# Splitting the attention probabilities in one operation per engine instead of two halves

## The chip, the core and the metric

The kernel runs on one core of one Trainium2 chip. The metric is device time in microseconds (us) of one execution, the median of several runs. Engines are called by the profile's names: PE (TensorE, matrix products), PEld (its weight loads), DVE (VectorE), ACT (ScalarE), POOL (GpSimd), SP (SyncE, here the queue that issues the DMAs).

## The reference, cut to what matters

64 graphs of 128 nodes with 512 features pass through two masked attentions with 8 heads (first nodes to edges, then edges to nodes, with the incidence matrix transposed and as it is), layer norms, a feed-forward network of width 2048 and a last layer norm:

```python
def _attn(q, k, v, mask):
    scores = jnp.einsum('bhid,bhjd->bhij', qh, kh) * SCALE
    scores = jnp.where(mask[:, None] > 0, scores, -jnp.inf)
    w = jax.nn.softmax(scores, axis=-1)
    out = jnp.einsum('bhij,bhjd->bhid', w, vh)
...
edge_features = _attn(eq, nk, nv, n2e_mask)
edge_features = _ln(edge_features + pe, norm1_g, norm1_b)
...
node_updates = _attn(nq, ek, ev, incidence_matrix)
node_features = _ln(pe + node_updates, norm2_g, norm2_b)
h = jax.nn.gelu(_lin(node_features, ffn_w1, ffn_b1), approximate=False)
out = _ln(node_features + _lin(h, ffn_w2, ffn_b2), norm3_g, norm3_b)
```

All of it is in float32. The kernel reaches the accuracy by splitting operands into a high and a low part and summing three (or five) products of the parts.

## The kernel before

The 64 graphs are worked on in 16 groups of 4. Each attention pass goes over the 16 groups, and each group takes 4 steps (`u` = 0 to 3): a step is one pair of heads for the 4 graphs, so a pass has 64 steps and the two passes 128, numbered n. The probabilities of a step are a 128x1024 tile: 8 blocks (4 graphs, 2 heads) of 128x128. Of the 16 groups of a pass the first two and the last two are written out, and the 12 between them run as 6 iterations of a loop of two groups, which is 8 steps (`over_groups`, L109). The feed-forward pass follows the two attention passes.

Every engine has its own program, and semaphores tie them. Nothing orders the work but these programs, each in the order in which it is written.

- PE in a step: keys, queries (24 products), the weighing of the values with the probabilities of two steps earlier (`weigh`, L861), transposes of the finished group (`turn`, L843), values (12 products, L877), and the scores of the step (L928), which need the split queries `q_lo`. One `weigh` of each group also waits for the low part of the values, which POOL makes.
- DVE in a step: the mask and the maximum of the 8 score blocks of the step before (`mask_and_maximum`, L766), the rest of a value (L742), once per group the centring of the norm (L684), the low part of the probabilities (`probabilities_low`, L775), the low parts of keys and queries (L747, L750, L755), and the sum of the weighed values with the tokens (`add_weighed`, L690 to L712).
- ACT in a step: 8 exponentials with the row sums (L526), the high part of the probabilities (`probabilities_high`, L533), high parts of keys and queries (L513 to L520), of the next group's source (L549), the copies of turned blocks (L483), the high part of a value (L509).
- POOL in a step: the middle and low part of a value (`value_low`: L627, L629), low parts of the source (L642), the bias of the tokens (`add_bias`, L647). Each of these reads SBUF.
- SP: `turn_probabilities` (L378 to L386) waits until the earlier step's probabilities are weighed, then until both halves of `p_hi` are there, and issues its transposing DMA; then the same for `p_lo`.

The split of the probabilities: `probs` (float32) is copied to `p_hi` (float16) by ACT, and DVE computes `p_lo = probs - p_hi`. Both are done in two halves of 128x512, and DVE may start its first half when ACT has made its first half:

```python
act.wait_ge(exped, UNIT * n + 4 * h + 4)
nc.scalar.copy(p_hi[:, 4 * h:4 * h + 4, :], probs[:, 4 * h:4 * h + 4, :]).then_inc(p_hi_ready, 1)
...
dve.wait_ge(p_hi_ready, 2 * n + h + 1)
nc.vector.tensor_tensor(p_lo[:, 4 * h:4 * h + 4, :], probs[:, 4 * h:4 * h + 4, :], p_hi[:, 4 * h:4 * h + 4, :],
                        ALU.subtract).then_inc(p_lo_ready, 1)
```

The first half's copy waits for the first 4 exponentials, the second's for all 8. In the loop over steps both halves come after all 8 exponentials; only after the last step of the second pass (`ends`) ACT runs 4 exponentials, a half, 4 exponentials, a half. `weights_high` of the feed-forward weights (`high`, L219) and their low parts (`low`, L226) are a copy and a subtraction of 128x1024 each.

Of the kernel before, what the change touches and what calls it, by code (L numbers as in the profile page):

```python
# [46 lines left out]
ALU = mybir.AluOpType  # L47
# [26 lines left out]
UNIT = GB * 2  # L74
# [5 lines left out]
def wait(engine, semaphore, value):  # L80

    if isinstance(value, int) and value <= 0:
        return
    engine.wait_ge(semaphore, value)
# [144 lines left out]
def attention_passes(nc, ctx, m, block, passes, feed_forward, nodes_features, residual, identity_in):  # L229
# [147 lines left out]
    def turn_probabilities(sp, n):  # L377

        wait(sp, weighed, n)
        sp.sem_inc(sp_steps, 1)  # L380
        sp.wait_ge(p_hi_ready, 2 * n + 2)
        sp.sem_inc(sp_steps, 1)
        sp.dma_start_transpose(pt_hi[:], p_hi[:].rearrange("p j i -> p (j i)")).then_inc(hi_turned, 16)
        sp.wait_ge(p_lo_ready, 2 * n + 2)
        sp.sem_inc(sp_steps, 1)
        sp.dma_start_transpose(pt_lo[:], p_lo[:].rearrange("p j i -> p (j i)")).then_inc(lo_turned, 16)  # L386

# [100 lines left out]
    def _(act):  # L488
# [37 lines left out]
                nc.scalar.activation(probs[:, j, :], probs[:, j, :], ACT.Exp, bias=minus_max[:, j:j + 1], scale=-1.0,  # L526
                                     accum_out=row_sum[:, side, j:j + 1]).then_inc(exped, 1)

        def probabilities_high(n, h):
            if h == 0:  # L530
                wait(act, hi_turned, 16 * n)
            act.wait_ge(exped, UNIT * n + 4 * h + 4)
            nc.scalar.copy(p_hi[:, 4 * h:4 * h + 4, :], probs[:, 4 * h:4 * h + 4, :]).then_inc(p_hi_ready, 1)  # L533

        def split_queries(g):

# [18 lines left out]
        def body(g, parity, before, own, after):  # L555
            if ends(g):
                n = C * g - 1
                for h in range(2):
                    exponentials(n, 1, h)
                    probabilities_high(n, h)  # L560
                feed_forward.high(act, 2)
                feed_forward.high(act, 3)
                return
            for u in range(C):
                n = C * g + u - 1
                first = starts(g) and u == 0
                if u == 2 and own != after:

                    act.wait_ge(projected, value_place(g, 3) + 1)
                    if after == 1:  # L570
                        weights_high(1, "v")
                    else:
                        feed_forward.high(act, 0)
                        feed_forward.high(act, 1)
                if u == 0 and starts(g):
                    value_high(0, 0, 0)
                    value_high(0, 0, 1)
                if not first:
                    exponentials(n, (u - 1) % 2, 0)
                    exponentials(n, (u - 1) % 2, 1)  # L580
                    probabilities_high(n, 0)
                    probabilities_high(n, 1)
                key_high(g, own, u)
                query_high(g, own, u)
                if u < 2:
                    split_source(g, parity, range(2 * u, 2 * u + 2))
                if u == 0 and not below(g, 2):
                    copy_turned(act, g - 2, own, 3)
                if u == 2 and not starts(g):
                    copy_turned(act, g - 1, before, 0)  # L590
                    copy_turned(act, g - 1, before, 1)
                if u == 3:
                    if own == 1 and after == 1:
                        split_queries(g + 1)
                    if not starts(g):
                        copy_turned(act, g - 1, before, 2)
                    if at(g, last_group - 1):
                        copy_turned(act, g - 1, before, 3)
                if u < 2:
                    value_high(g, parity, u + 2)  # L600
                elif not at(g, last_group - 1):
                    value_high(g + 1, 1 - parity, u - 2)
            if own != after and after == 1:

                weights_high(1, "k")
                weights_high(1, "q")
                split_queries(g + 1)
# [107 lines left out]
    def _(dve):  # L715
# [42 lines left out]
        def mask_and_maximum(n, first):  # L758
            if first is not None:
                dve.wait_ge(mask_ready, first + 1)  # L760
            wait(dve, p_lo_ready, 2 * n)
            for h in range(2):
                gate(dve, scored, 2 * n + h + 1, dve_scratch[:, h:h + 1])
                for j in range(4):
# [3 lines left out]
                        in1=mask[:, 2 * h + j // 2, :], scale=-SCALE, scalar=LARGEST, op0=ALU.add, op1=ALU.min,  # L768
                        accum_out=minus_max[:, 4 * h + j:4 * h + j + 1]).then_inc(masked, 1)

        def probabilities_low(n, h):
            if h == 0:
                wait(dve, lo_turned, 16 * n)
            dve.wait_ge(p_hi_ready, 2 * n + h + 1)
            nc.vector.tensor_tensor(p_lo[:, 4 * h:4 * h + 4, :], probs[:, 4 * h:4 * h + 4, :], p_hi[:, 4 * h:4 * h + 4, :],  # L775
                                    ALU.subtract).then_inc(p_lo_ready, 1)

        def first_queries():

# [5 lines left out]
        def body(g, parity, before, own, after):  # L785
            if ends(g):
                n = C * g - 1
                mask_and_maximum(n, None)
                for h in range(2):
                    probabilities_low(n, h)  # L790
                feed_forward.low(dve, 2)
                feed_forward.low(dve, 3)
                return
            for u in range(C):
# [18 lines left out]
                if u == 2 and not starts(g):  # L813
                    centre(dve, g - 1, 1 - parity)
                if not first:
                    probabilities_low(n, 0)
                    probabilities_low(n, 1)
                key_low(g, own, u)
                query_low(g, own, u)
                if u == 2 and own != after:  # L820
# [607 lines left out]
```

## Time and profile before

| | us |
|---|---|
| median of 3 runs | 2949.8 (2947.25 to 2950.87) |
| the profiled execution | 2950.69 |
| its span (first to last instruction) | 2948.9 |
| around the span | 1.8 |
| attention passes, from the trace's start | 0 to about 1525 |

The granted TensorE clock was 0.994 of full speed over the span. Busy times are in the first part of the profile's page; the wait views say which engine stood idle before an instruction, and what ended it; the timeline view lists instructions with start and length, equal neighbours merged (`x2`), and in brackets the idle time just before them.

### The profile page before, as it was taken

The numbers are of one execution on the slowest core, as the hardware profiler recorded it, in microseconds if no ns is written. First come the engines' busy times: TensorE is split into PE (matmuls) and PEld (weight loads), VectorE is DVE, ScalarE is ACT, GpSimd is POOL, SyncE is SP. The second block draws the span as 40 slices with busy tenths as digits, with TensorE's granted clock in tenths as the row PEclk, the third lists the DMA queues.
The fourth block names the chain that finished last, engine by engine and source line by source line (L and its number), as shares of the span: only waits on it lengthen the run. The fifth ranks groups of instructions, "written<-read, shape, count | busy, mean of one in ns | idle before, by whom it ended". The sixth has DMA issues, their size and how long they took to land.

```text
span 2948.9 us, 54948 instructions
## 1 busy us (share of the span) xinstructions
PE 2864.6 (97%) x17920; PEld 2393.6 (81%) x17920; DVE 1761.7 (60%) x5972; ACT 1551.1 (53%) x4138; POOL 1118.1 (38%) x1115
## 2 busy tenths in 40 slices
PE   9999999999899999999979999999999999999997
PEld 7888877888788888888868888888888888888886
DVE  7888888888888888888873333322333332233333
ACT  6777777777787787787864222222222222222221
POOL 3443534344355645546522322333312333321233
PEclk9999999999999999999999999999999999999998
DMA  7554444444566766756664101011101011110101
GB/s 198 125 115 120 118 111 118 114 125 109 149 151 157 180 162 157 175 147 168 162 170 134 57 29 53 33 57 57 57 30 55 33 52 57 57 57 28 58 14 57
DMA packets 487992, 295.43 MB, mean 100 GB/s; under 512 B 278912, under 2 KB 410112, under 8 KB 487808
## 3 DMA queue, kind: packets, MB, share of 16 engines
q1 hardware_dynamic: 487808, 293.49, 37.5%
q14 instruction: 131, 1.07, 0.1%
q8 instruction: 53, 0.87, 0.1%
HBM read 159.21 MB, written 67.11 MB: 77 GB/s over the span
## 4 chain that ended last, share of the span: by engine, by line
PE 80%; DVE 8%; issue 5%; ACT 4%; POOL 1%; DMA 0%; DVEq 0%; SPq 0%; ACTq 0%; POOLq 0%
PE proj L1326 23%; PE proj L877 23%; PE score L1340 12%; PE proj L1340 12%; PE score L928 4%; PE att_out L861 4%; ACT att_probs L526 2%; DVE normed L703 2%; PE att_turn L843 2%; ACT turned L483 1%; DVE att_p_lo L775 1%; DVE att_q_lo L755 1%; DVE att_stats L708 1%; DVE att_k_lo L750 1%; ACT att_p_hi L533 0%
## 5 line engine op out<-in xcount | busy, mean ns | idle before, releaser
L1259 DVE TENSOR_TENSOR hidden_lo<-hidden,hidden_hi 128x512 fp32r<-128x512 f32 x256 | 188.2, 735 | 935.0 <-ACT hidden_hi L1111 935.0
L1118 ACT ACTIVATE hidden<-proj,ffn_bias 128x512 f32<-128x512 f32 x256 | 176.8, 691 | 996.3 <-PE proj L1326 996.3
L526 ACT ACTIVATE att_probs<-att_probs,att_minus_max 128x128 f32<-128x128 f32 x1024 | 397.7, 391 | 169.8 <-DVE att_minus_max L766 169.8
L775 DVE TENSOR_TENSOR att_p_lo<-att_probs,att_p_hi 128x512 f16<-128x512 f32 x256 | 232.5, 947 | 150.1 <-ACT att_p_hi L533 150.1
L101 POOL TENSOR_TENSOR pool_scratch<-pool_scratch 128x1 f32<-128x1 f32 x144 | 38.1, 264 | 698.5 <-DVE ffn_moments L1199 396.4
L1178 POOL TENSOR_TENSOR source_lo<-source_raw,source_hi 128x512 fp32r<-128x512 f32 x60 | 79.3, 1322 | 449.6 <-ACT source_hi L1129 449.6
L766 DVE CUSTOM_DVE_ANT_0 att_probs<-score,att_mask 128x128 f32<-128x128 f32 x1024 | 226.7, 287 | 18.8 <-PE score L928 9.7
L877 PE MATMUL proj<-weight_v_hi,source_hi 128*128 128x512 f32 x512 | 216.1, 422 | 9.9 <-DVE weight_v_lo L724 7.2
L483 ACT ACTIVATE turned<-att_turn,att_shift,att_gain 128x128 f32<-128x128 f32 x512 | 193.0, 458 | 59.2 <-PE att_turn L843 59.2
L642 POOL TENSOR_TENSOR source_lo<-source_raw,source_hi 128x512 fp32r<-128x512 f32 x128 | 163.0, 1296 | 126.7 <-ACT source_hi L549 126.7
L877 PE MATMUL proj<-source_hi,weight_k_hi 128*128 128x512 f32 x512 | 201.0, 393 | 2.3 <-DVE weight_k_lo L724 2.3
L877 PE MATMUL proj<-weight_v_hi,source_lo 128*128 128x512 f32 x512 | 202.4, 395 | 0.0
L877 PE MATMUL proj<-weight_v_lo,source_hi 128*128 128x512 f32 x512 | 201.2, 393 | 0.0
L877 PE MATMUL proj<-source_lo,weight_k_hi 128*128 128x512 f32 x512 | 200.7, 392 | 0.0
L877 PE MATMUL proj<-source_hi,weight_k_lo 128*128 128x512 f32 x512 | 199.3, 389 | 0.0
L1326 PE MATMUL proj<-source_hi,w_lo 128*128 128x512 f32 x512 | 199.2, 389 | 0.0
L1326 PE MATMUL proj<-source_hi,w_hi 128*128 128x512 f32 x512 | 199.2, 389 | 0.0
L1326 PE MATMUL proj<-source_lo,w_hi 128*128 128x512 f32 x512 | 199.2, 389 | 0.0
L526 ACT ACTIVATION_READ_ACCUMULATOR att_probs<-att_probs,att_minus_max 128x1 f32 x1024 | 193.0, 188 | 0.0
L861 PEld LDWEIGHTS att_out<-att_v,att_pt_hi 128*128 128x128 f16 x3072 | 149.2, 98 | 44.5 <-issue 44.5
L647 POOL TENSOR_TENSOR att_tokens<-att_tokens,bias_row 128x512 f32<-128x512 f32 x128 | 181.4, 1417 | 1.0 <-DMA att_tokens<-in_x 1.0
L861 PE MATMUL att_out<-att_v,att_pt_hi 128*128 128x64 bf16 x3072 | 163.9, 193 | 9.1 <-POOL att_v L629 9.1
(149 smaller groups left out, 8358.9 us busy)
## 6 DMA issues: line engine op xcount, KB each, us to landing
att_tokens<-in_x SPq DMA_DIRECT2D x128, 256.0 KB, 3.0
edges_t<-turned SPq DMA_DIRECT2D x64, 256.0 KB, 2.5
source_raw<-edges_t SPq DMA_DIRECT2D x16, 1024.0 KB, 6.1
att_query_raw<-in_x_t SPq DMA_DIRECT2D x16, 1024.0 KB, 6.8
nodes_t<-turned SPq DMA_DIRECT2D x64, 256.0 KB, 2.8
source_raw<-nodes_t SPq DMA_DIRECT2D x16, 1024.0 KB, 6.1
normed<-nodes SPq DMA_DIRECT2D x16, 1024.0 KB, 5.6
ffn_weight_raw<-in_x SPq DMA_DIRECT2D x16, 1024.0 KB, 8.1
```

Source lines behind the costliest of these rows:

```text
L483: last = nc.scalar.activation(turned[:, b % 2, c, :], turn_bank[:, c * P:(c + 1) * P], ACT.Identity, bias=shift_column[own][:, c:c + 1], s ...
L526: nc.scalar.activation(probs[:, j, :], probs[:, j, :], ACT.Exp, bias=minus_max[:, j:j + 1], scale=-1.0, accum_out=row_sum[:, side, j:j + 1 ...
L642: nc.gpsimd.tensor_tensor(source_lo[1 - parity][:, c, :], source_raw[:, c, :], source_hi[1 - parity][:, c, :].bitcast(F32), ALU.subtract). ...
L647: nc.gpsimd.tensor_tensor(pair(tokens, u), pair(tokens, u), bias_v[:, u * P:(u + 1) * P].rearrange("p (o d) -> p o d", o=1).to_broadcast([ ...
L766: nc.vector.tensor_tensor_reduce(out=probs[:, 4 * h + j, :], in0=score_bank[h][:, j * P:(j + 1) * P], in1=mask[:, 2 * h + j // 2, :], scal ...
L775: nc.vector.tensor_tensor(p_lo[:, 4 * h:4 * h + 4, :], probs[:, 4 * h:4 * h + 4, :], p_hi[:, 4 * h:4 * h + 4, :], ALU.subtract).then_inc(p ...
L861: last = nc.tensor.matmul(out, p, value, start=(i == 0), stop=(i == len(products) - 1))
L877: last = nc.tensor.matmul(bank[:], stationary, moving, start=(c == 0 and i == 0), stop=(c == C - 1 and i == 2))
L1118: nc.scalar.activation(hidden[:, c % 2, :], up_bank[c % 2][:], ACT.Gelu, bias=bias_1[:, c:c + 1]).then_inc(activated, 1)
L1259: nc.vector.tensor_tensor(hidden_lo[:, c % 2, :], hidden[:, c % 2, :], hidden_hi[:, c % 2, :].bitcast(F32), ALU.subtract).then_inc(hidden_ ...
L1326: last = nc.tensor.matmul(up_bank[c % 2][:], w, s, start=(i == 0), stop=(i == len(products) - 1))
L1340: last = nc.tensor.matmul(down_bank[b][:], h, w, start=(c == 0 and i == 0), stop=(c == FC - 1 and i == 2))
```

## The change

The copy to `p_hi` becomes one 128x1024 operation on ACT, and the subtraction one 128x1024 operation on DVE. Each semaphore counts one per step instead of two, and all waits on them are renumbered. The copy waits for all 8 exponentials; the subtraction waits for the whole copy. In `ends` all 8 exponentials now come ahead of the copy.

```diff
-        sp.wait_ge(p_hi_ready, 2 * n + 2)
+        sp.wait_ge(p_hi_ready, n + 1)
...
-        sp.wait_ge(p_lo_ready, 2 * n + 2)
+        sp.wait_ge(p_lo_ready, n + 1)
...
-        def probabilities_high(n, h):
-            if h == 0:
-                wait(act, hi_turned, 16 * n)
-            act.wait_ge(exped, UNIT * n + 4 * h + 4)
-            nc.scalar.copy(p_hi[:, 4 * h:4 * h + 4, :], probs[:, 4 * h:4 * h + 4, :]).then_inc(p_hi_ready, 1)
+        def probabilities_high(n):
+
+            wait(act, hi_turned, 16 * n)
+            act.wait_ge(exped, UNIT * n + UNIT)
+            nc.scalar.copy(p_hi[:], probs[:]).then_inc(p_hi_ready, 1)
...
                 for h in range(2):
                     exponentials(n, 1, h)
-                    probabilities_high(n, h)
+                probabilities_high(n)
...
-                    probabilities_high(n, 0)
-                    probabilities_high(n, 1)
+                    probabilities_high(n)
...
-            wait(dve, p_lo_ready, 2 * n)
+            wait(dve, p_lo_ready, n)
...
-        def probabilities_low(n, h):
-            if h == 0:
-                wait(dve, lo_turned, 16 * n)
-            dve.wait_ge(p_hi_ready, 2 * n + h + 1)
-            nc.vector.tensor_tensor(p_lo[:, 4 * h:4 * h + 4, :], probs[:, 4 * h:4 * h + 4, :], p_hi[:, 4 * h:4 * h + 4, :],
-                                    ALU.subtract).then_inc(p_lo_ready, 1)
+        def probabilities_low(n):
+
+            wait(dve, lo_turned, 16 * n)
+            dve.wait_ge(p_hi_ready, n + 1)
+            nc.vector.tensor_tensor(p_lo[:], probs[:], p_hi[:], ALU.subtract).then_inc(p_lo_ready, 1)
...
-                for h in range(2):
-                    probabilities_low(n, h)
+                probabilities_low(n)
...
-                    probabilities_low(n, 0)
-                    probabilities_low(n, 1)
+                    probabilities_low(n)
```

## Rows read from the trace of the kernel before

**Rows 1.** The page's first part: busy us (share of the span) xinstructions.

```profile
PE 2864.6 (97%) x17920; PEld 2393.6 (81%) x17920; DVE 1761.7 (60%) x5972; ACT 1551.1 (53%) x4138; POOL 1118.1 (38%) x1115
```

**Rows 2.** Waits of DVE, 40 to 590 us: us in total, times, longest us.

```profile
DVE att_p_lo L775 <- ACT att_p_hi L533: 53.6, 35, 1.8
DVE att_dve_scratch L92 <- issue: 15.1, 5, 3.1
```

**Rows 3.** Waits of PE, 40 to 590 us.

```profile
PE score L928 <- DVE att_q_lo L755: 11.3, 5, 2.4
PE att_out L861 <- POOL att_v L629: 3.7, 4, 0.9
```

**Rows 4.** Waits of PE, 960 to 1400 us.

```profile
PE att_out L861 <- POOL att_v L629: 4.6, 5, 0.9
...
PE score L928 <- DVE att_q_lo L755: 3.0, 5, 0.7
```

**Rows 5.** Groups by line and form, 100 to 1620 us: xcount | busy us, mean ns.

```profile
L533 ACT CAST att_p_hi<-att_probs 128x512 f16<-128x512 f32 x242 | 136.6, 612 | 0.1
...
L219 ACT CAST w_hi<-ffn_weight_raw 128x1024 fp32r<-128x1024 f32 x10 | 10.5, 1047 | 1.6 <-DMA ffn_weight_raw<-in_w 1.6
...
L226 DVE TENSOR_TENSOR weight_k_lo<-ffn_weight_raw,weight_k_hi 128x1024 fp32r<-128x1024 f32 x2 | 2.5, 1225 | 1.0 <-ACT weight_k_hi L219 0.9
```

**Rows 6.** Timeline of ACT, a step of the loop and the last step: start us, us.

```profile
212.30 0.19 ACT L526 ACTIVATION_READ_ACCUMULATOR att_probs<-att_probs,att_minus_max 128x1 f32 x1
212.39 1.13 ACT L533 CAST att_p_hi<-att_probs 128x512 f16<-128x512 f32 x2
...
1522.68 0.19 ACT L526 ACTIVATION_READ_ACCUMULATOR att_probs<-att_probs,att_minus_max 128x1 f32 x1
1522.90 0.62 ACT L533 CAST att_p_hi<-att_probs 128x512 f16<-128x512 f32 x1
```

**Rows 7.** Timeline of DVE and POOL, first pass, steps 16 to 19 and 23.

```profile
213.10 1.46 DVE L775 TENSOR_TENSOR att_p_lo<-att_probs,att_p_hi 128x512 f16<-128x512 f32 x2 [1.76 <-ACT att_p_hi L533]
...
218.61 1.29 POOL L647 TENSOR_TENSOR att_tokens<-att_tokens,bias_row 128x512 f32<-128x512 f32 x1
...
225.13 1.45 POOL L647 TENSOR_TENSOR att_tokens<-att_tokens,bias_row 128x512 f32<-128x512 f32 x1
...
225.37 2.36 DVE L775 TENSOR_TENSOR att_p_lo<-att_probs,att_p_hi 128x512 f16<-128x512 f32 x2
...
236.68 2.55 DVE L775 TENSOR_TENSOR att_p_lo<-att_probs,att_p_hi 128x512 f16<-128x512 f32 x2 [1.76 <-ACT att_p_hi L533]
...
236.95 1.73 POOL L647 TENSOR_TENSOR att_tokens<-att_tokens,bias_row 128x512 f32<-128x512 f32 x1
...
248.18 1.93 DVE L775 TENSOR_TENSOR att_p_lo<-att_probs,att_p_hi 128x512 f16<-128x512 f32 x2 [1.29 <-ACT att_p_hi L533]
...
297.36 2.27 DVE L775 TENSOR_TENSOR att_p_lo<-att_probs,att_p_hi 128x512 f16<-128x512 f32 x2 [0.75 <-ACT att_p_hi L533]
...
297.51 1.57 POOL L629 TENSOR_TENSOR att_v<-att_v_rest,att_v 128x512 bf16<-128x512 f32 x1
```

**Rows 8.** Timeline of DVE, second pass, steps 86 to 88.

```profile
1039.19 0.29 DVE L766 CUSTOM_DVE_ANT_0 att_probs<-score,att_mask 128x128 f32<-128x128 f32 x1 [0.20 <-issue]
...
1043.33 1.30 DVE L775 TENSOR_TENSOR att_p_lo<-att_probs,att_p_hi 128x512 f16<-128x512 f32 x2 [1.75 <-ACT att_p_hi L533]
...
1057.24 2.17 DVE L775 TENSOR_TENSOR att_p_lo<-att_probs,att_p_hi 128x512 f16<-128x512 f32 x2 [1.47 <-ACT att_p_hi L533]
...
1068.36 1.46 DVE L775 TENSOR_TENSOR att_p_lo<-att_probs,att_p_hi 128x512 f16<-128x512 f32 x2 [1.76 <-ACT att_p_hi L533]
```

**Rows 9.** Timeline of DVE and PE between the passes, and SP after the last step.

```profile
748.75 2.49 DVE L724 TENSOR_TENSOR weight_v_lo<-att_weight_v_raw,weight_v_hi 128x512 fp32r<-128x512 f32 x4
...
749.54 0.47 PE L877 MATMUL proj<-weight_v_hi,source_hi 128*128 128x512 f32 x1 [2.77 <-issue]
...
1529.50 1.35 SPq L213 DMA_DIRECT2D ffn_weight_raw<-in_w  x2
```

## The prediction

> **What bounds the kernel now.** I read the shares first, then the waits of DVE and PE in stretches of the attention passes, then single steps in the timeline. PE is busy for 97% of the span [rows 1], so PE looks like the only bound. The waits say otherwise for the first pass. From 40 to 590 us DVE waits for nothing but ACT's copy `p_hi` (35 times, 53.6 us) and a pause at each turn of the loop, 5 times up to 3.1 us [rows 2]; no row says that it waits for PE. ACT's exponentials in turn start on DVE's maxima. So here DVE and ACT run a ring of their own: maxima, exponentials, `p_hi`, `p_lo`, `k_lo`, `q_lo`, `add_weighed`, the next maxima. PE follows it: once in each turn of the loop it waits for `q_lo` (5 times, 11.3 us) and once more for POOL's `att_v`, which starts from DVE's `v_rest` (4 times, up to 0.9 us) [rows 3]. What the ring loses in 8 steps, PE loses at its next such wait. In the second pass the same two waits come 5 times each, but shorter (3.0 and 4.6 us) [rows 4], and DVE does wait for scores: at 1039.19 for 0.20 us [rows 8] (the row says issue, but this is the first use of a score bank). There only what is lost after the last such wait counts.
>
> **What the change removes, adds and moves.** Per step it takes away one ACT and one DVE instruction and the overlap between the engines.
>
> ACT. The pair of copies takes 1.13 us [rows 6], one 128x1024 copy to a 4-byte type 1.05 [rows 5]; I take that for the float16 copy, since the 128x512 copy costs 0.61 [rows 5] and two of them overlap by 0.09. Saved: 0.08. But the copy now waits for the last exponential, whose row sum is read out at the end. Without that wait the first copy starts 0.09 after the start of the readout (212.30, 212.39); where the wait was there already, after the last step, 0.22 (1522.68, 1522.90) [rows 6]. Added: 0.13. So `p_hi` is whole 0.05 later than before. Behind it on ACT stand `k_hi`, `q_hi`, the source's high part and the copies of turned blocks, 0.05 later each; SP's first transposition already waited for both halves and is 0.05 later too. No row has PE waiting for a transposition [rows 3, 4], so that costs nothing.
>
> DVE. Two undisturbed halves take 1.30 us (1043.33) [rows 8], one 128x1024 subtraction 1.225 [rows 5]: 0.07 saved. But `p_lo` starts later: before, the copy's start + 0.61 + 0.10 = 0.71 (212.39 to 213.10) [rows 5 to 7]; now 0.13 + 1.05 + 0.10 = 1.28 after it, so 0.57 later. With nothing in the way it ends at 0.57 + 1.22 = 1.79 after the old start, against 1.30: 0.49 late. Behind it on DVE stand `k_lo`, `q_lo`, `add_weighed` and the next maxima, and PE's scores wait for `q_lo`.
>
> POOL changes this from step to step. At 225.37 DVE was late for other reasons; POOL's addition (225.13 to 226.58) kept the pair until 227.73 [rows 7], 1.15 after POOL's end. One operation then ends 1.15 - 0.07 = 1.08 after POOL's end. In the loop of the first pass the 8 steps are:
> - Steps 16 and 20 (213.10): the pair took 1.46, slowed by a POOL operation that is over by the new start. New end 1.79: +0.33 each.
> - Steps 17 and 21 (225.37): `p_hi` is long there. -0.07 each.
> - Steps 18 and 22 (236.68): POOL's addition starts 0.27 after the old start and fell between the halves; the pair took 2.55. It now starts before `p_lo` asks, runs its undelayed 1.29 (218.61) to 1.56, and `p_lo` ends at 2.64: +0.09 each.
> - Step 19 (248.18): POOL is still at work when `p_lo` asks. -0.07.
> - Step 23, at the loop's turn (297.36): POOL's subtraction starts 0.15 after the old start. It took 1.57, about 0.4 of it behind the first half, so 1.17 undelayed: 0.15 + 1.17 + 1.08 = 2.40 against 2.27 [rows 7], +0.13; the same step of other rounds starts at a slightly other place and comes out near 0. I take +0.06.
>
> Together 0.66 - 0.14 + 0.18 - 0.07 + 0.06 = 0.69 us in 8 steps. The ring has no wait on PE, so it adds up: five rounds of 8 (steps 8 to 47) 3.45, the steps 1 to 7 by the same rules 0.5, and step 48, whose delay PE meets at `att_v`, 0.33: **4.3 us**.
>
> Rows show POOL's addition stretched from 1.29 to 1.73 behind a half, and DVE's second half stopped behind that addition [rows 7]. By the Trainium skill ("SBUF — State Buffer", Who interferes with whom) the two engines share a port pair that one instruction keeps to its end, which speaks against longer operations: a POOL operation that comes second waits up to 1.22 us instead of 0.6. The trace agrees; by it the sum stays as it is, since in the steps above POOL comes first.
>
> Between the passes PE waits 2.77 us for `weight_v_lo`, whose first quarter DVE ends 0.1 earlier [rows 9]. DVE's steps 49 to 61 gather about 1.1, nearly all of it in steps 56 and 60, where no POOL operation is in the way (+0.49 each); one wait for a score of 0.2 on the way swallows its part: **+0.9**.
>
> Second pass, five rounds. Since the last wait for a score, DVE gathers +0.33 and +0.09 less 0.07 in steps 83 to 85, of which the 0.20 of that wait [rows 8] swallows all but 0.15; step 86 (1043.33) has no POOL in it, +0.49; step 87 (1057.24) about 0; step 88 (1068.36) +0.33, met at `att_v`. 0.97 a round, **4.8 us**.
>
> Last steps: three late `p_lo` of 0.49 with waits between them leave about 0.7; the last step's exponentials, no longer split by a copy, give back 0.3; SP's loads of feed-forward weights at 1529.50 [rows 9] follow: **+0.4**. The feed-forward pass has none of these operations.
>
> Sum: 4.3 + 0.9 + 4.8 + 0.4 = 10.4 us on the profiled 2950.69 (span 2948.9 and 1.8 around it), 2961.1; the median is 0.9 lower, so **2960 us**.
>
> Bounds: if the readout wait costs nothing, open steps lose 0.20 (0.36 without POOL), and the same sum gives about 6.4 us, 2956. If it costs 0.05 more, and the step at the turn loses 0.13 in every round, about 13, 2963. The pause at the turn of the loop, up to 3.1 us [rows 2], is a stop after a branch, and DVE's loop body gets shorter; I allow 0.2 us a turn either way, 2 us over ten turns.
>
> **Rivals.**
> *The slack takes it (no change).* If the ring is pulled back to PE in every group, only the ten waits for `q_lo` [rows 3, 4] count, at about 0.33 each: 3 us, 2953. For it: PE's 97%. Against it: no wait for a score in 550 us of the first pass [rows 2].
> *POOL loses its place (faster).* If POOL's operations at steps 18, 22 and 23 came after `p_lo` asks (later than 0.57 after the old start), the whole operation would run undisturbed and end at 1.79 instead of 2.55 and 2.27: -0.76 twice and -0.48, so a round is 0.69 - 0.18 - 0.06 - 2.0 = -1.55, the first pass about -9; with +2.5 in the second pass (step 87 likewise) and 1.3 at the hand-offs, -5 to -6: 2944. Against it: POOL starts at 0.27 and 0.15 [rows 7], and follows DVE's `v_rest`, not `p_hi`.
> *Instructions saved, nothing lost.* 128 x 0.15 us saved would be up to 19 us; it needs `p_lo` to start where it did, which the new wait forbids. I give it almost nothing.
>
> **How the numbers follow.** A difference under 0.2% (5.9 us) can't be told from no change. Forecast 0.70, the slack 0.19, POOL 0.08, others 0.03. The forecast's own range is 2954 to 2965 with the pause's 2 us; down to 2952 takes in the slack's 2953. Faster by over 0.2% is half of POOL's case and the last rival: 0.06. Within: the slack, the rest of POOL's case and the forecast's low end: 0.25. Slower: 0.69.
>
> **What would show it.** `p_lo` waiting for `p_hi` about 0.57 us longer each time it waits, at 1.22 us or behind POOL; `p_hi` 0.22 after the last readout's start, at 1.05; PE's waits for `q_lo` and `att_v` together about 4 us longer in the first pass and 5 in the second, 0.33 of it at each `att_v`. Wrong if the waits for `q_lo` stay as they are, if POOL's addition comes after `p_lo` at step 18, or if the pause at the loop's turn moves by more than 0.3.

## The result, and the profile after

The changed kernel takes **2958.5 us** in the median of 8 runs (2957.22 to 2961.45), the kernel before 2950.55 in 8 runs beside it (2947.25 to 2952.66): a ratio of **1.003 [1.002, 1.004]**, 8 us slower. The profiled execution took 2957.61 us with a span of 2955.6, so its span is 6.7 us longer than before. The lines that follow are from the profile of the changed kernel; each group of before to which they answer is named.

The page's first part [rows 1]:

```profile
PE 2868.5 (97%) x17920; PEld 2396.0 (81%) x17920; DVE 1720.0 (58%) x5844; ACT 1550.1 (52%) x4010; POOL 1106.7 (37%) x1115
```

DVE is busy for 41.7 us less and ACT for 1.0 us less, with 128 instructions fewer on each, and the kernel is slower. Most of DVE's 41.7 us is not saved work. The merged subtraction is 0.07 us shorter than two undisturbed halves (1.23 against 1.30 [rows 8]), which makes 9 us in 128 steps. The rest is time in which a half waited behind POOL and counted as busy; now DVE is idle instead, as the idle time before the subtraction shows (140.1 us before, 195.8 after).

Groups by line and form, 100 to 1620 us (xcount | busy us, mean ns | idle before) [rows 5]; the first line is of the kernel before:

```profile
L775 DVE TENSOR_TENSOR att_p_lo<-att_probs,att_p_hi 128x512 f16<-128x512 f32 x242 | 218.7, 942 | 140.1 <-ACT att_p_hi L533 140.1
...
L774 DVE TENSOR_TENSOR att_p_lo<-att_probs,att_p_hi 128x1024 f16<-128x1024 f32 x121 | 178.8, 1478 | 195.8 <-ACT att_p_hi L533 195.8
...
L533 ACT CAST att_p_hi<-att_probs 128x1024 f16<-128x1024 f32 x121 | 126.6, 1046 | 10.8 <-ACT att_probs L526 0.4
```

Timeline of ACT in step 16, the last readout and the copy (start us, us) [rows 6]:

```profile
212.99 0.19 ACT L526 ACTIVATION_READ_ACCUMULATOR att_probs<-att_probs,att_minus_max 128x1 f32 x1
213.26 1.05 ACT L533 CAST att_p_hi<-att_probs 128x1024 f16<-128x1024 f32 x1
```

The copy takes the 1.05 us that was forecast. It starts 0.27 after the start of the last readout, where the first half started 0.09 after a readout: a copy that waits for the last row sum starts 0.18 us later.

Timeline of DVE and POOL in steps 16 to 19 [rows 7]; the bracket is the idle time before:

```profile
214.41 1.23 DVE L774 TENSOR_TENSOR att_p_lo<-att_probs,att_p_hi 128x1024 f16<-128x1024 f32 x1 [2.38 <-ACT att_p_hi L533]
...
226.44 2.29 DVE L774 TENSOR_TENSOR att_p_lo<-att_probs,att_p_hi 128x1024 f16<-128x1024 f32 x1
...
238.31 2.02 DVE L774 TENSOR_TENSOR att_p_lo<-att_probs,att_p_hi 128x1024 f16<-128x1024 f32 x1 [2.38 <-ACT att_p_hi L533]
...
237.96 1.28 POOL L646 TENSOR_TENSOR att_tokens<-att_tokens,bias_row 128x512 f32<-128x512 f32 x1
...
249.90 1.23 DVE L774 TENSOR_TENSOR att_p_lo<-att_probs,att_p_hi 128x1024 f16<-128x1024 f32 x1 [1.92 <-ACT att_p_hi L533]
```

In steps 16 and 18 DVE waits 0.62 us longer for `p_hi` (2.38 against 1.76). At step 18 POOL's addition still comes first, and `p_lo` ends 1.09 us after it (239.24 to 240.33). All four steps go as forecast, to 0.05 us.

Waits of DVE, 40 to 590 us (us in total, times, longest) [rows 2], all that the view lists:

```profile
DVE att_p_lo L774 <- ACT att_p_hi L533: 80.0, 36, 2.4
DVE att_dve_scratch L92 <- issue: 14.4, 5, 3.1
```

Waits of PE, 40 to 590 us [rows 3]:

```profile
PE score L924 <- DVE att_q_lo L754: 9.1, 5, 2.1
PE att_out L857 <- POOL att_v L628: 7.0, 9, 1.3
```

Waits of PE, 960 to 1400 us [rows 4]:

```profile
PE att_out L857 <- POOL att_v L628: 7.4, 9, 1.3
...
PE score L924 <- DVE att_q_lo L754: 3.2, 5, 1.4
```

PE's waits for `q_lo` did not grow (9.1 us against 11.3, and 3.2 against 3.0); those for `att_v` did, and come 9 times instead of 4 and 5. Between the passes [rows 9], DVE and PE:

```profile
751.27 1.28 DVE L723 TENSOR_TENSOR weight_v_lo<-att_weight_v_raw,weight_v_hi 128x512 fp32r<-128x512 f32 x2
...
752.06 0.76 PE L873 MATMUL proj<-weight_v_hi,source_hi 128*128 128x512 f32 x1 [3.63 <-issue]
```

PE's wait grew from 2.77 to 3.63, by 0.86.

The one place of the first pass that did not go as forecast is the step at the loop's turn. First the kernel before: the third and last row of the view from which rows 2 come, and the timeline of DVE in step 23 (it goes on with the `p_lo` at 297.36 and POOL's subtraction at 297.51 [rows 7]):

```profile
DVE att_mask L806 <- DVE att_minus_max L766: 2.5, 5, 0.6
```

```profile
295.59 0.43 DVE L806 TENSOR_SCALAR att_mask<-att_adj 128x512 f32<-128x512 f32 x1 [0.58 <-DVE att_minus_max L766]
295.93 0.68 DVE L742 TENSOR_TENSOR att_v_rest<-proj,att_v 128x512 f32<-128x512 f32 x1
```

and the changed kernel, DVE and POOL in the same step:

```profile
296.48 0.43 DVE L803 TENSOR_SCALAR att_mask<-att_adj 128x512 f32<-128x512 f32 x1
296.82 0.68 DVE L741 TENSOR_TENSOR att_v_rest<-proj,att_v 128x512 f32<-128x512 f32 x1
...
299.42 1.23 DVE L774 TENSOR_TENSOR att_p_lo<-att_probs,att_p_hi 128x1024 f16<-128x1024 f32 x1 [1.92 <-ACT att_p_hi L533]
...
298.40 1.16 POOL L628 TENSOR_TENSOR att_v<-att_v_rest,att_v 128x512 bf16<-128x512 f32 x1
```

Before, DVE stands still for 0.58 us ahead of the mask, with its own last maximum as the only releaser: a second stop of DVE's program, about 2 us after the pause at the loop's turn. It comes at all five turns, 2.5 us in all. After, the mask follows the maxima at once. `v_rest` and POOL's subtraction come 0.55 us earlier, counted from the step's first maximum. That subtraction used to fall between the halves, and now ends at 299.56, 0.14 after `p_lo` has started, without stretching it. `p_lo` runs its undisturbed 1.23 us.

Worked out from both traces, the end of `p_lo` counted from the first maximum of its step, after less before, in us:

| step | forecast | measured |
|---|---|---|
| 16, 20: POOL just out of the way | +0.33 | +0.38 |
| 17, 21: DVE late for other reasons | -0.07 | -0.07, -0.07 |
| 18, 22: POOL's addition first | +0.09 | +0.09, +0.07 |
| 19 | -0.07 | -0.08 |
| 56, 60, 86: no POOL | +0.49 | +0.52 to +0.55 |
| 15, 23, 31, 39, 47: loop's turn, first pass | +0.06 | -0.41, -0.42, -0.41, -0.41, -0.41 |
| 79, 87, 95, 103, 111: loop's turn, second pass | about 0 | -0.29, -0.93, -1.02, -0.43, -0.42 |

### The profile page after: what moved, and what is told of

It is laid out like the page before. It is cut to its first block, busy times and chain, and to the rows that moved or that the text cites. A ratio compares the mean times of both kernels' runs of the same rounds, so it can differ in the third digit from the quotient of the medians.

```text
span 2955.6 us, 54548 instructions
## 1 busy us (share of the span) xinstructions
PE 2868.5 (97%) x17920; PEld 2396.0 (81%) x17920; DVE 1720.0 (58%) x5844; ACT 1550.1 (52%) x4010; POOL 1106.7 (37%) x1115
## 3 DMA queue, kind: packets, MB, share of 16 engines
q14 instruction: 124, 1.02, 0.1%
## 4 chain that ended last, share of the span: by engine, by line
PE 72%; DVE 11%; ACT 8%; issue 7%; POOL 2%; DMA 1%; DVEq 0%; SPq 0%; ACTq 0%; POOLq 0%
PE proj L1322 23%; PE proj L873 17%; PE score L1336 12%; PE proj L1336 12%; ACT att_probs L526 4%; PE score L924 3%; PE att_out L857 3%; DVE normed L702 2%; DVE att_q_lo L754 2%; PE att_turn L839 1%; DVE att_stats L707 1%; ACT att_p_hi L533 1%; ACT turned L483 1%; DVE att_even_sum L702 1%; DVE att_k_lo L749 1%
## 5 line engine op out<-in xcount | busy, mean ns | idle before, releaser
L774 DVE TENSOR_TENSOR att_p_lo<-att_probs,att_p_hi 128x1024 f16<-128x1024 f32 x128 | 189.6, 1481 | 209.5 <-ACT att_p_hi L533 209.5
L646 POOL TENSOR_TENSOR att_tokens<-att_tokens,bias_row 128x512 f32<-128x512 f32 x128 | 168.7, 1318 | 0.6 <-DMA att_tokens<-in_x 0.5
```

Of the source, the lines that this page charges most:

```text
L646: nc.gpsimd.tensor_tensor(pair(tokens, u), pair(tokens, u), bias_v[:, u * P:(u + 1) * P].rearrange("p (o d) -> p o d", o=1).to_broadcast([ ...
L774: nc.vector.tensor_tensor(p_lo[:], probs[:], p_hi[:], ALU.subtract).then_inc(p_lo_ready, 1)
```

## The experiments

Ratios are to runs of the kernel before on the same chip (medians 2950.16 to 2950.82). Where a shift is given "up to" a place, it is worked out from the traces: the start of the same score matmul, less its start before. The three places lie at 635.36, 886.40 and 1412.82 us before (just behind the first pass's loop, at the start and near the end of the second pass's); the last column goes to the last instruction.

| kernel | up to 635 | to 886 | to 1413 | to the end | sum |
|---|---|---|---|---|---|
| changed kernel | +1.7 | +0.8 | +3.9 | +0.4 | +6.8 |
| copy whole, subtraction in halves | +8.9 | +3.4 | +8.6 | +3.2 | +24.1 |
| copy in halves, subtraction whole | +2.0 | -1.5 | +0.4 | +1.2 | +2.2 |
| halves, copy waits for all exponentials | +2.2 | -0.3 | -0.3 | +2.1 | +3.7 |
| halves without overlap | +6.0 | +1.2 | +7.3 | +1.4 | +15.9 |
| before, statistics moved | -18.5 | -0.3 | -8.8 | +1.4 | -26.1 |
| changed, statistics moved | -17.4 | -0.3 | -3.0 | -1.0 | -21.7 |
| changed, one more instruction | +4.2 | +1.0 | +4.9 | +0.6 | +10.7 |

### Which part of the change costs

**1. Only the overlap taken away.** Copies and subtractions stay halves; the first subtraction waits for both copies.

```
-            dve.wait_ge(p_hi_ready, 2 * n + h + 1)
+            dve.wait_ge(p_hi_ready, 2 * n + 2)
```

> Both splits in halves as before, but the first half of the subtraction waits for both halves of the copy: only the overlap is taken away, no operation is merged. Theory: p_lo starts 0.52 us later, so nearly the change's loss, 5 to 9 us: 2956 to 2960. Rival (merging operations costs, by POOL's port or by the readout wait): near the kernel before, 2950 to 2952.

Measured: 2966.59 us (2964.52 to 2967.72), 1.0054 [1.0041, 1.0068], 7 us above the theory's range. The overlap is worth 16 us, twice what the whole change costs: merging gives some back.

**2. Only the wait for all exponentials.** Halves, with their overlap; each copy waits for the step's eighth exponential.

```
-            act.wait_ge(exped, UNIT * n + 4 * h + 4)
+            act.wait_ge(exped, UNIT * n + UNIT)
...
                 for h in range(2):
                     exponentials(n, 1, h)
+                for h in range(2):
                     probabilities_high(n, h)
```

> Both splits in halves as before, but the first half of the copy also waits for all 8 exponentials (and in the last step all exponentials come first, as in the change). Theory: p_hi and p_lo 0.17 us later each step; of that, steps with a POOL operation in the way keep none, so 2 to 4 us slower than before: 2952 to 2955. Rival (the lost overlap is the whole cost): 2950 to 2951.

Measured: 2954.36 (2952.17 to 2956.1), 1.0013 [1.0004, 1.0022], 4.0 us slower and within the theory's range, though the interval's low end is close to no change. `p_lo` starts 0.19 to 0.20 later in most steps. But the table puts only 2.2 us into the first pass, nothing into the second, and 2.1 behind 1413 us, where the last steps' order is changed too. So this run backs the theory for the first pass alone.

**3. Only the subtraction merged.**

```
+            for h in range(2):
+                act.wait_ge(exped, UNIT * n + 4 * h + 4)
+                nc.scalar.copy(p_hi[:, 4 * h:4 * h + 4, :], probs[:, 4 * h:4 * h + 4, :]).then_inc(p_hi_ready, 1)
...
+            dve.wait_ge(p_hi_ready, 2 * n + 2)
+            nc.vector.tensor_tensor(p_lo[:], probs[:], p_hi[:], ALU.subtract).then_inc(p_lo_ready, 1)
```

> ACT copies in two halves as before, DVE subtracts in one operation after both. Theory: p_lo starts 0.52 instead of 0.62 us later, so about 1 us faster than the change and 6 to 7 slower than the kernel before: 2955.5 to 2958.5 us, and p_lo starts 1.23 us after the first copy's start. Rival (the copy's wait for the last exponential's readout is the cost): near the kernel before, 2950 to 2952.

Measured: 2954.3 (2952.63 to 2957.18), 1.0014 [1.0004, 1.0023], between the two expectations. Against experiment 1's kernel, which differs in the form of the subtraction and in the order of the very last step, merging it is worth **12.3 us**. Against the changed kernel, the copy in halves is worth 4.2 us. That is the size of experiment 2's 4.0, but not at the same places: here the gain lies behind 635 us (2.0 against 1.7 up to there), so the two do not confirm each other.

**4. Only the copy merged.**

```
+            act.wait_ge(exped, UNIT * n + UNIT)
+            nc.scalar.copy(p_hi[:], probs[:]).then_inc(p_hi_ready, 1)
...
+            dve.wait_ge(p_hi_ready, n + 1)
+            for h in range(2):
+                nc.vector.tensor_tensor(p_lo[:, 4 * h:4 * h + 4, :], ...
```

> ACT copies in one operation, DVE subtracts in two halves, both after the whole copy. Theory (the cost is that p_lo starts about 0.62 us later, after the whole copy, in a ring of DVE and ACT that PE follows): as slow as the change or 1 to 4 us slower still, since the pair of halves takes 1.28 instead of 1.22 us: 2958 to 2963 us. Rival (the long operation on DVE costs, because it holds the port that POOL needs): near the kernel before, 2950 to 2953.

Measured: 2973.0 (2972.4 to 2974.96), 1.0076 [1.0062, 1.009], slower than either expectation. With the copy merged, merging the subtraction too is worth 14.5 us. Two halves without overlap take 1.29 us against 1.23, so 0.07 in each step. That is not enough; the rest is at the loop's turn. Here it is in experiment 1's kernel, DVE and POOL in step 23:

```profile
298.54 0.43 DVE L806 TENSOR_SCALAR att_mask<-att_adj 128x512 f32<-128x512 f32 x1 [0.72 <-DVE att_minus_max L766]
...
300.69 2.08 DVE L775 TENSOR_TENSOR att_p_lo<-att_probs,att_p_hi 128x512 f16<-128x512 f32 x2 [1.13 <-ACT att_p_hi L533]
...
300.46 1.17 POOL L629 TENSOR_TENSOR att_v<-att_v_rest,att_v 128x512 bf16<-128x512 f32 x1
```

The second stop is there (0.72), POOL's subtraction starts 0.23 before `p_lo` asks, and the pair takes 2.08 in place of 1.23. In the first pass the kernel before and the three of experiments 1, 2 and 4, with two subtractions per step, stand idle for 0.43 to 0.72 us ahead of the mask at each of the five turns; the changed kernel and that of experiment 3, with one, for 0.03 or 0.04. The `p_lo` of experiment 1's kernel ends later than the changed kernel's by some 0.07 in five steps of 8 and by 0.48 to 0.75 at the turn, and 0.03 earlier in two: 0.9 us in 8 steps, 4.6 in five rounds. Measured up to 635 us: 6.0 - 1.7 = 4.3. Why the merged copy with halves loses 6 us more than experiment 1's kernel is only partly seen (its `p_lo` ends 0.10 later where POOL is not in the way); the rest stays open.

### What decides the stop at the loop's turn

**5. The count on the semaphore.** The merged subtraction counts up by two, so that DVE's wait is again for 2n.

```
-            wait(dve, p_lo_ready, n)
+            wait(dve, p_lo_ready, 2 * n)
...
-...ALU.subtract).then_inc(p_lo_ready, 1)
+...ALU.subtract).then_inc(p_lo_ready, 2)
```

> The changed kernel, but its subtraction counts its semaphore up by two and the waits on it are for 2n and 2n + 2, as before the change; the instructions on data stay as they are. It asks what took away VectorE's second stop at the loop's turn (0.25 to 0.39 us at the tile of the mask in the first pass before, 0.03 after). If it is the arithmetic of that wait, the stop is back, GpSimd's value operation comes some 0.4 us later at the five turns of the first pass, and the time is 2959 to 2964 us. If it is that the loop's code is a subtraction shorter per step, nothing changes: 2957 to 2960, no stop over 0.1 us there.

Measured: 2958.41 (2955.53 to 2959.56), 1.0028 [1.0016, 1.004], and at the turns of the first pass DVE is idle for 0.03 or 0.04 us ahead of the mask. The arithmetic of the wait is not the cause. (The stop before is 0.44 to 0.58 us by the idle time of the timeline, not the 0.25 to 0.39 of the expectation.)

**6. One more instruction per step.** A memset of one unused column, ahead of the subtraction.

```
                 if not first:
+                    nc.vector.memset(dve_scratch[:, 2 + GB:3 + GB], 0.0)
                     probabilities_low(n)
```

> The changed kernel with one more VectorE instruction per step (a memset of one column, 59 ns by the rows of the gate's memsets) in VectorE's idle time ahead of the subtraction, so that each pass of the loop holds as many VectorE instructions as before the change. If the second stop at the loop's turn hangs on how many instructions the loop's code holds, it is back (0.2 to 0.5 us at the tile of the mask in the first pass) and the time is 2959 to 2964 us. If not, the memset is hidden and the time is 2957 to 2960.

Measured: 2961.38 (2958.91 to 2962.96), 1.0034 [1.0022, 1.0046], 2.9 us over the changed kernel in medians; the intervals overlap, so the traces have to tell. DVE and POOL in step 23:

```profile
297.92 0.43 DVE L803 TENSOR_SCALAR att_mask<-att_adj 128x512 f32<-128x512 f32 x1 [0.42 <-DVE att_minus_max L765]
...
298.89 0.06 DVE L813 MEMSET att_dve_scratch<- 128x1 f32 x1
...
300.48 1.62 DVE L774 TENSOR_TENSOR att_p_lo<-att_probs,att_p_hi 128x1024 f16<-128x1024 f32 x1 [1.52 <-ACT att_p_hi L533]
...
299.84 1.17 POOL L628 TENSOR_TENSOR att_v<-att_v_rest,att_v 128x512 bf16<-128x512 f32 x1
```

The memset itself is hidden (DVE idles for 1.52 us behind it), but the stop is back at all five turns of the first pass (0.42 to 0.56 us), ahead of an operation that runs before this step's memset does. POOL's subtraction is late again and `p_lo` is stretched to 1.62. At those turns `p_lo` ends 0.40 to 0.53 later than in the changed kernel, 2.2 us in all. Up to 635 us the kernel lies 2.5 behind it.

So the stop hangs on the code of the loop. Whether it is the amount of code or the place where it lies is not shown, and two things speak for the place. In the second pass, whose loop has the same steps, no kernel has this stop. And the kernel before with the statistics moved (experiment 8), which has as many DVE instructions as the kernel before (5972), does not stop ahead of the mask but one instruction later, ahead of `v_rest`, for 0.16 to 0.88 us. The row of DVE's waits there, 40 to 590 us:

```profile
DVE att_v_rest L747 <- issue: 2.8, 5, 0.9
```

**7. The price of a late `v_rest` alone.**

```
                     if not first:
+                        nc.vector.memset(filler[:], 0.0)
                         value_rest(g, parity, 1)
```

> The changed kernel with a memset of 128x512 ahead of the value rest at the loop's turn alone (no row shows such a memset; the mask's operation of that size takes 427 ns), in a stretch that ends in 1.85 us of VectorE's idle time. It holds GpSimd's value operation back by about as much as the lost stop let it come earlier (0.47 us or so). If the gain of 0.41 us at each turn of the first pass came from GpSimd finishing before the subtraction asks, that gain is gone where the operation now reaches into it or behind it: p_lo or the value operation is stretched at the turn, and the time is 2959 to 2964 us. Rival, the order at the turn is worth nothing: 2957 to 2960.

Measured: 2967.39 (2966.59 to 2969.09), 1.0057 [1.0044, 1.0071]. The expectation has a mistake: this place is the first step of every group, twice per pass of the loop, not the turn alone; the memset ran 31 times. Step 23:

```profile
299.58 0.48 DVE L806 MEMSET att_filler<- 128x512 f32 x1
...
302.04 1.72 DVE L775 TENSOR_TENSOR att_p_lo<-att_probs,att_p_hi 128x1024 f16<-128x1024 f32 x1 [1.44 <-ACT att_p_hi L534]
...
301.51 1.17 POOL L629 TENSOR_TENSOR att_v<-att_v_rest,att_v 128x512 bf16<-128x512 f32 x1
```

No second stop is there, and the 0.48 us are spent in idle time, but POOL moves into `p_lo`, which takes 1.72 instead of 1.23. `p_lo` starts as long after the step's first maximum as in the changed kernel (4.76 us) and ends some 0.49 later. With this at the first steps of all groups, the kernel is 8.9 us slower than the changed one. When POOL comes, and not DVE's own time, is what counts there.

### Whether the ring is what loses

**8. The statistics moved, in both kernels and in that of experiment 3.** In three steps of four, the statistics instructions go from the end of the step to the idle time ahead of `p_lo`. The first expectation counts two of 282 ns in a step; the timeline shows four, which overlap and take 0.87 us together. The statistics in the kernel before, ahead of step 16, then the statistics and `p_lo` of step 16 with the move:

```profile
208.16 0.87 DVE L708 BATCH_NORM_STATS2 att_stats<-normed 128x6 f32<-128x128 f32 x4
```

```profile
207.66 0.86 DVE L690 BATCH_NORM_STATS2 att_stats<-normed 128x6 f32<-128x128 f32 x4
209.49 1.46 DVE L780 TENSOR_TENSOR att_p_lo<-att_probs,att_p_hi 128x512 f16<-128x512 f32 x2 [0.97 <-ACT att_p_hi L533]
```

DVE's idle time ahead of `p_lo` falls from 1.76 [rows 7] to 0.97, so the move takes 0.79 us from the ring's path in such a step.

```
+    def statistics(dve, g, parity, u):
+        n = C * g + u
+        for b in range(GB):
+            dve.wait_ge(summed, n + 1)
+            nc.vector.bn_stats(stats[:, b, u, :], total[parity][:, b, u * P:(u + 1) * P]).then_inc(stats_ready, 1)
...
+                if u < 2 and not starts(g):
+                    statistics(dve, g - 1, 1 - parity, u + 1)
+                if u == 3:
+                    statistics(dve, g, parity, 0)
                 if not first:
                     probabilities_low(n, 0)
```

> The two halves are kept. In three steps of four the two statistics instructions (282 ns each) leave the stretch between the split and the next step's maxima and stand in VectorE's idle time ahead of the first subtraction. If the ring of VectorE and ScalarE sets TensorE's waits in the attention stages (11.3 + 3.7 us for the queries' rest and for the values in 40 to 590 us, 3.0 + 4.6 in 960 to 1400), 0.42 us less per step takes most of them but the ones at the loop's turn: 2935 to 2946 us. Rival, the ring's length is slack and only the loop's turn and the value wait count: 2948 to 2952.

> The changed kernel with the same move. If the change lost its time in the ring (+0.38 to +0.55 us per step in which the split ends later), the move gives it back and more: 2938 to 2950 us, and about as long as the other kernel with the move, since the steps then have slack for both forms. Rival, the loss lies outside the ring: 2955 to 2960.

> ScalarE's copies in halves, VectorE's subtraction in one, and the statistics in the idle time. If the parts add up (the copy in halves is worth some 4 us against the changed kernel, the move 10 or more), 2932 to 2944 us, the fastest of the four. Rival, once the ring has slack the form of the split is free: within 2 us of the other two kernels with the move. Where the clock falls after the wait at the loop's turn, as it did at five turns of this kernel without the move, up to 8 us of that are lost again.

Measured: before with the move **2924.53** (2923.71 to 2926.59), **0.9918 [0.9905, 0.9932]**; the changed kernel with it 2927.28 (2926.43 to 2929.22), 0.9925 [0.9912, 0.9939]; the kernel of experiment 3 with it 2926.98 (2923.31 to 2928.01), 0.992 [0.9906, 0.9933]. The first beats both kernels, by 26 and 34 us. The only wait of PE that its trace lists, from 40 to 590 us:

```profile
PE att_turn L853 <- ACT turned L483: 4.1, 11, 0.4
```

PE no longer waits for `q_lo` or `att_v` there: 11.3 + 3.7 us of before [rows 3] are gone, and 3.0 + 4.6 in the second pass [rows 4]. That is 22.6 of the 25.6 us, and no work was removed: DVE is busy for 1757.1 us against 1761.7 [rows 1]. DVE's waits now name PE's scores, 8.6 us at the five turns of the first pass. So the ring sets the time in the attention passes. The move gave 10 us more than the fast end of my first expectation, and 11 more than that of the second: they went by 0.42 us a step, three quarters of two instructions, where the trace gives three quarters of 0.79, some 0.6. With slack in the ring the two forms of the split differ by 2.8 us in place of 8. Of the third kernel the rival is nearer: with the move the three lie within 2.8 us, and the parts of the split no longer add up.

### The clock at the turn

**9. The kernel of experiment 3, started 2 us later.** The traces of that kernel and of the changed one differ in TensorE's clock after the wait for `q_lo` at the loop's turn. Stretches of the kernel of experiment 3 (PE, PEld, DVE, ACT and POOL busy, then the granted clock, DMA share, GB/s), and its wait:

```profile
303.40:306.70 3.30, 3.30 (x15) 3.10 (x14) 3.27 (x24) 1.63 (x8) 2.25 (x2) 0.50 0.36 98
```

```profile
303.02 0.39 PE L925 MATMUL score<-att_k_hi,att_q_hi 128*128 128x256 f32 x1 [1.98 <-DVE att_q_lo L755]
```

The same stretch of the changed kernel:

```profile
303.40:306.70 3.30, 3.30 (x21) 2.92 (x20) 3.27 (x24) 1.74 (x8) 2.29 (x2) 1.00 0.41 113
```

After a wait of 1.98 us the clock is at 0.50, 1.2 GHz, and 15 matmuls go through where 21 went at 2.4 GHz. It fell so at five turns, after waits of 1.89 to 2.15 us; at none of these turns did it fall in the kernel before, after waits of 2.11 to 2.37 us, or in the changed kernel, after 1.40 to 2.13. I had put up to 8 us on these falls (experiment 8's last expectation).

```
+        for c in range(4):
+            place = filler[:, c, :] if c < 2 else early_lo[:, 512 * (c - 2):512 * (c - 1)]
+            nc.vector.tensor_tensor(place, weight_raw["k"][:, c, :], wh["k"][:, c, :].bitcast(F32), ALU.subtract)
         weights_low(0, "q")
```

> The kernel with ScalarE's copies in halves and VectorE's subtraction in one, with four more subtractions (0.62 to 0.69 us each) on VectorE ahead of the queries' weights at the start, 0.6 us of them in its idle time: everything after starts some 2 us later. In that kernel the granted clock fell after the wait at five turns of the loop, while before the change waits of the same length left it alone. If the length of the wait decides, the five falls stay and the time is 2 us longer, 2955 to 2958 us. If it hangs on when the wait comes, the falls are gone at most turns and the time is 2946 to 2953 in spite of the later start.

Measured: 2958.79 (2956.5 to 2959.75), 1.0026 [1.0016, 1.0037]. The clock now falls at two of the five turns (305 and 209 us). At another, after a wait as long as that above, it does not:

```profile
400.90:404.20 3.30, 3.06 (x19) 2.81 (x20) 3.23 (x20) 1.57 (x5) 2.84 (x3) 1.00 0.46 114
```

```profile
401.14 0.38 PE L930 MATMUL score<-att_k_hi,att_q_hi 128*128 128x256 f32 x1 [1.88 <-DVE att_q_lo L760]
```

So the length of the wait alone does not decide. But three falls fewer gave no time back: the kernel starts 2.27 us later and is 2.9 us later at 635 us. Neither expectation fits. PE follows the ring of DVE and ACT in this pass, so slower matmuls behind the wait are probably covered; a run in which only the clock differs is missing. The further 1.6 us in the medians come later: the traces have this kernel's shift grow by 3.8 us against that of experiment 3 between 635 and 1413 us, and shrink by 1.3 behind that. Why is open.

## Why the prediction was right, point by point

Forecast 2960.0, range 2952 to 2965, slower; measured 2958.5. The mechanism is the one forecast: the merged split ends later in the steps where POOL is out of the way, and this adds up in the ring of DVE and ACT. Experiment 1 shows that the lost overlap does it, experiment 8 that the ring is the bound. Against its own execution the sum was 10.4, and 6.9 was measured; in the medians 8.0. That the median lies 1.5 us from the forecast is partly luck, since two of the sum's terms came out otherwise:

- **ACT.** "0.13" for the readout wait: 0.18. "1.05" for the copy: 1.05.
- **DVE.** "0.57 later", 0.62 measured; the classes of steps hold to 0.06 us (table above).
- **What DVE waits for.** "DVE waits for nothing but ACT's copy `p_hi` ... and a pause at each turn" was read wrong: the same view has a third row, 5 waits of up to 0.6 us ahead of the mask, which rows 2 leave out. It is the second stop, and the term below was mis-sized for want of it.
- **First pass, 4.3 us.** Measured +1.7. The term that failed is "Step 23, at the loop's turn ... I take +0.06": it is -0.41, in all five rounds. 0.47 x 5 = 2.4 of the missing 2.6 us. The prediction had "I allow 0.2 us a turn either way" for a shorter loop body, and "if the pause at the loop's turn moves by more than 0.3" as a sign of error. That pause takes 14.4 us in five against 15.1 [rows 2], with one of the five 0.49 shorter. The -0.41, which is there at all five turns, comes from the second stop behind the pause: 0.58 us ahead of 295.59, gone with one DVE instruction less per step, and back with one more (experiment 6).
- **Between the passes, +0.9.** Measured +0.86 at PE's wait.
- **Second pass, 4.8 us.** Measured +3.9, but not by the steps of the sum. The turn gained 0.29 to 1.02 instead of "about 0", 3.1 us over five turns. Little of this reached PE: its five waits for `q_lo` at these turns were only 0.54 to 0.67 us long before, and at best (1065.28 and 1159.29) they fell to 0.25. The five old waits for `att_v` grew from 0.91 to 1.30, near the "0.33 of it at each `att_v`". Four new ones of 0.21 to 0.23 us, at steps 85, 93, 101 and 109, were not in the sum. Together PE's two kinds of waits grew by 3.0 us there [rows 4], the rest of the 3.9 is not traced. At two of the turns `p_lo` now goes first, and POOL's value operation waits for it (no wait of PE is for these two operations). DVE and POOL in step 87:

```profile
1061.79 1.23 DVE L774 TENSOR_TENSOR att_p_lo<-att_probs,att_p_hi 128x1024 f16<-128x1024 f32 x1 [0.77 <-ACT att_p_hi L533]
...
1061.92 2.13 POOL L628 TENSOR_TENSOR att_v<-att_v_rest,att_v 128x512 bf16<-128x512 f32 x1
```

  POOL's 1.16 us have become 2.13, since `p_lo` holds on until 1063.02. The Trainium skill ("SBUF — State Buffer", Who interferes with whom) says that the order of issue, and not the form of the operation, decides who blocks; rows of one kernel agree, with `p_lo` at 1.23 undisturbed and 2.02 behind POOL, and POOL's subtraction at 1.16 and 2.13.
- **The end, +0.4.** Measured +0.4, which may be chance: that column runs from -1.0 to +3.2 us among the kernels, and does not follow how late their `p_lo` is.
- **The signs.** "PE's waits ... about 4 us longer in the first pass and 5 in the second": 1.1 and 3.0. "Wrong if the waits for `q_lo` stay as they are": they did not grow, so by this sign the path was wrong in part. What the sum had PE lose at `q_lo`, it lost at `att_v`.
- **The rivals.** "The slack takes it" fell: without the overlap the loss is 16 us, and with 0.79 us less in three steps of four the kernel gains 26. "POOL loses its place" did not come at steps 18 and 22 (POOL at 237.96, `p_lo` at 238.31), but it did at turns of the second pass, at 1061.79. "Instructions saved, nothing lost" fell with DVE's wait, 80.0 us against 53.6.

Merging has a gain of its own: without it the same loss of overlap costs 16 us, with it 8. In the first pass this gain is 4.3 us, the stop with what it does to POOL's place and 0.07 us in most steps; I had priced only the latter.

## What to carry to other kernels

Before two operations on different engines are merged, look at whether their halves overlap: here the overlap was worth 16 us, and merging gave half of it back. Find the ring that the engines run among themselves (an engine with idle time that waits only for one partner, while the busiest engine waits for that pair once in a while); what shortens the ring counts, even by moving 0.79 us from its path into its idle time, which gave three times what the change had cost. Read a view of waits to its last row: the one that was left out here held the largest error. In a loop, read the step at the turn separately, since here one instruction more or less per step decided whether DVE stopped there, and with it whether DVE or POOL came first.

## What was not expected of the hardware

- A stop of DVE's program about 2 us behind the pause at the loop's turn, with 0.42 to 0.72 us of idle time ahead of the mask, that comes and goes with one instruction per step elsewhere in the loop. It is there at all first-pass turns of the kernel before, of those of experiments 1, 2 and 4, and of the one with a subtraction and a memset; ahead of the mask DVE is idle for only 0.03 or 0.04 us in the kernels with one subtraction. With two subtractions and the statistics moved it lies ahead of `v_rest` instead (0.16 to 0.88). In the second pass no kernel shows it. The traces suggest a load of code: the queue named `instruction` moves 8 KB at every turn 2.7 to 3.0 us after the step's first maximum in the kernels that stop ahead of the mask, and 3.0 to 3.2 after it in the changed kernel and those of experiments 3, 5 and 7, which do not. No run varied the place of the code alone.
- A copy on ACT that follows an exponential with a row sum starts 0.27 us after the readout's start if it needs it, against 0.09 if not.
- The granted clock fell to 1.2 GHz after waits of 1.89 to 2.15 us at five turns, and stayed at 2.4 GHz after one of 1.88 in another kernel, at all five turns of the changed one, and at all five of the kernel before, whose waits were longer (2.11 to 2.37). In the kernels of experiments 1, 4, 6 and 7 it fell at two or three first-pass turns each, in those of 2 and 5 at one. What decides was not found.
